# Two copies ahead of the gelu, and a step of the recurrence ahead of two maxima, in a macaron layer on eight cores

## The reference

```python
# x: (16, 4096, 1024); w1: (4096, 1024), w2: (1024, 4096), Wa, Wx: (1024, 1024)
def bitlinear(x, w, b):                  # int8 activations, ternary weights
    return einsum('bsd,fd->bsf', act_quant(rmsnorm(x)), weight_quant(w)) + b
def ffn(x):
    return bitlinear(gelu(bitlinear(x, w1, b1)), w2, b2)
def attn(x):                             # a gated linear recurrence
    rt, it = sigmoid(x @ Wa.T + ba), sigmoid(x @ Wx.T + bx)
    a = exp(-8 * softplus(-Lam) * rt)
    b = sqrt(1 - a * a) * (it * x)
    return scan(h = a * h + b)           # over the 4096 tokens
x = x + 0.5 * ffn(layernorm(x))
x = x + attn(layernorm(x))
x = x + 0.5 * ffn(layernorm(x))
```

## Time and profile before

| | us |
|---|---|
| three runs | 5005.6, 4954.83, 4643.77 |
| their median | 4954.83 |
| the profiled execution | 4643.38 |
| its span, slowest core (core 2) | 4641.8 |
| spans of its cores | 4631.0 to 4641.8 |
| PE busy in the span | 4225.2 (91%) |
| DVE busy | 3528.0 (76%) |
| ACT busy | 2790.7 (60%) |
| POOL busy | 972.4 (21%) |
| mean granted TensorE clock | 0.963 |

### The profile page before, as it was taken

One profiled execution on the slowest core, in us unless ns is written; L12 is line 12 of the kernel. 1 busy time (PEld: TensorE's weight loads), 2 busy tenths in 40 slices (PEclk: granted clock), 3 DMA queues, 4 the chain that ended last, 5 costly groups with the idle time before them and its releaser, 6 DMA issues.

```text
span 4641.8 us, 75615 instructions; the slowest of 8 cores (4631.0 to 4641.8 us)
## 1 busy us (share of the span) xinstructions
PE 4225.2 (91%) x23463; PEld 2242.4 (48%) x23463; DVE 3528.0 (76%) x4614; ACT 2790.7 (60%) x3464; POOL 972.4 (21%) x1541
## 2 busy tenths in 40 slices
PE   1699999999999989999999999999999999999999
PEld 0344455555555545454545445555555555444444
DVE  4888777777777777777777777777777777777786
ACT  4555666666666666666666666666666666555553
POOL 0122222222222222222221212222122221222221
PEclk9999999999999999999999999999999999999999
DMA  9455655556555555565555565555556555455555
GB/s 287 153 168 161 203 186 177 182 186 198 184 187 186 177 182 182 188 193 191 186 177 180 181 193 183 197 186 181 177 182 197 185 195 177 147 186 172 167 188 181
DMA packets 366185, 857.59 MB, mean 185 GB/s; under 512 B 39368, under 2 KB 45664, under 8 KB 365664
## 3 DMA queue, kind: packets, MB, share of 16 engines
q1 hardware_dynamic: 365792, 852.76, 56.5%
HBM read 740.41 MB, written 112.20 MB: 184 GB/s over the span
## 4 chain that ended last, share of the span: by engine, by line
PE 70%; DVE 16%; issue 7%; ACT 3%; DMA 2%; SPq 1%; DVEq 0%; POOL 0%; ACTq 0%; POOLq 0%
PE f_pm L486 29%; PE f_po L642 27%; PE aux L874 9%; DVE f_h L499 3%; PE aux L463 2%; DVE w2T L932 2%; DVE w2T L923 2%; ACT f_A L470 2%; DMA p_ring<-L_ffn_w 2%; PE aux L946 1%; DVE f_col L510 1%; PE aux L850 1%; DVE f_q L540 1%; SPq L62 1%; DVE f_col L435 1%
## 5 line engine op out<-in xcount | busy, mean ns | idle before, releaser
L486 PE MATMUL f_pm<-w1T,f_q1T 128*128 128x512 fp8e4 x8192 | 1837.6, 380 | 13.7 <-DVE f_h L499 4.7
L486 PEld LDWEIGHTS f_pm<-w1T,f_q1T 128*128 128x128 f16 x8192 | 795.0, 98 | 924.7 <-issue 24.1
L642 PE MATMUL f_po<-w_x,f_A 128*128 128x512 fp8e4 x4960 | 1161.9, 389 | 3.9 <-DMA w_x<-w2x 2.2
L505 ACT ACTIVATE f_h<-f_h 128x1024 f32<-128x1024 f32 x512 | 539.5, 1057 | 865.0 <-DVE f_h L499 859.6
L499 DVE SCALAR_TENSOR_TENSOR f_h<-f_pm,f_col,f_b1c 128x1024 f32<-128x1024 f32 x512 | 654.8, 1279 | 222.2 <-PE f_pm L486 217.1
L669 DVE SCALAR_TENSOR_TENSOR f_xb<-f_po,f_col,f_xb 128x512 f32<-128x512 f32 x496 | 370.1, 748 | 583.7 <-PE f_po L642 557.4
L642 PEld LDWEIGHTS f_po<-w_x,f_A 128*128 128x128 f16 x4960 | 498.2, 101 | 569.6 <-issue 60.4
L510 DVE TENSOR_REDUCE f_col<-f_h 128x1 f32<-128x1024 f32 x512 | 621.5, 1214 | 29.1 <-ACT f_h L505 17.1
L874 PE MATMUL aux<-w2T,g_w 128*128 128x256 bf16 x4096 | 536.0, 290 | 110.9 <-ACT f_A L470 110.9
L517 ACT ACTIVATE f_sqj<-f_h 128x1024 bf16<-128x1024 f32 x512 | 540.4, 1056 | 26.0
L874 PEld LDWEIGHTS aux<-w2T,g_w 128*128 128x128 bf16 x4096 | 418.6, 103 | 214.3 <-issue 119.2
(11 more groups left out here) (102 smaller groups left out, 3855.0 us busy)
## 6 DMA issues: line engine op xcount, KB each, us to landing
w_x<-w2x SPq DMA_DIRECT2D x1736, 256.0 KB, 5.3
g_w<-wg SPq DMA_DIRECT2D x256, 512.0 KB, 5.7
p_ring<-L_ffn_w SPq DMA_DIRECT2D x64, 512.0 KB, 16.4
f_xb<-L_attn_x SPq DMA_DIRECT2D x64, 512.0 KB, 6.1
xs<-f_xb SPq DMA_DIRECT2D x64, 512.0 KB, 6.4
g_xg<-xs SPq DMA_DIRECT2D x32, 1024.0 KB, 8.1
xs<-g_xg SPq DMA_DIRECT2D x32, 1024.0 KB, 5.2
f_xb<-xs SPq DMA_DIRECT2D x64, 512.0 KB, 5.6
```

The costliest lines, as they stand in the source:

```text
L486: a = put("tensor", lambda t, k=k, hf=hf, o=o: t.matmul(pm[i][:, hf * 512:(hf + 1) * 512], q1T[:, k * 128:(k + 1) * 128], w1T[:, o:o + 512 ...
L505: tj["gelu%d" % p] = put("scalar", lambda s: s.activation(hg[:, sl], hg[:, sl], AF.Gelu), waits=[ev])
L642: a = put("tensor", lambda t, k=k, c=c, w=w: t.matmul(po[:, bank * 512:(bank + 1) * 512], lhs[:, k * 128:(k + 1) * 128], w[:, c * 512:(c + ...
```

## The change

Three calls are moved in the loop over `j`. No instruction is added, removed or altered.

- `t2(pre, order[0])` stands before `evict1(cur, 1)`; it stood after it and after `recur(j, -4)`, which has VectorE work only. On TensorE its transposes follow `mm1(cur, 1)` as they did. On ScalarE its copy is ahead of gelu 1, where it was behind it.
- `t2(pre, order[1])` stands before `evict1(cur, 2)`; it stood after it, after `product_out(K, 3)` and after `gmax(cur, 1)`. On TensorE its transposes follow `mm1(cur, 2)` as they did. On ScalarE its copy is ahead of gelu 2, where it was behind it.
- `recur(j, -1)` stands before `gmax(cur, 2)`, `gmax(cur, 3)` and `scale2(cur)`, which are VectorE's alone. TensorE's and ScalarE's orders are as they were; on VectorE the addition of `g_tr_out` in stage 0 is ahead of the two maxima and the scale.

```diff
                         if cur is not None:
                             mm1(cur, 1)
+                        if pre is not None:
+                            t2(pre, order[0])
+                        if cur is not None:
                             evict1(cur, 1)
                         recur(j, -4)
-                        if pre is not None:
-                            t2(pre, order[0])
                         if nxt is not None:
                             quant1(nxt)
                         recur(j, -3)
...
                         if cur is not None:
                             gmax(cur, 0)
                             mm1(cur, 2)
+                        if pre is not None:
+                            t2(pre, order[1])
+                        if cur is not None:
                             evict1(cur, 2)
                         if odd:
                             product_out(K, 3)
                         if cur is not None:
                             gmax(cur, 1)
-                        if pre is not None:
-                            t2(pre, order[1])
-                        if cur is not None:
                             mm1(cur, 3)
                             evict1(cur, 3)
+                        recur(j, -1)
+                        if cur is not None:
                             gmax(cur, 2)
                             gmax(cur, 3)
                             scale2(cur)
-                        recur(j, -1)
```

## The result

The changed kernel takes 4369.8 us (median of four runs; three of them lie between 4368.5 and 4370.0), 0.941 of the kernel before, with a 95% interval of 0.9387 to 0.9432. The profiled execution took 4369.6 us, against 4643.4 us before: 273.8 us less, or 5.9%. The median of the four runs of before is 4799 us because two of them, like one of the changed kernel (4950.6 us, with a mean granted clock of 0.85 on four cores), ran at a lower clock, and no comparison here uses those.

The account below looks back on a forecast made before the run. TensorE was taken as the bound, losing time to waits and the lower clock behind them. Gains of 5.8 + 4.2 + 1.5 + 4.6 = 16.1 us a cycle, 16 cycles, 258 us: 4643 to 4385 us; 8-in-10 range 4320 to 4490.

Parts of the forecast that it names:

- the basis of the time: Whole kernel: gain subtracted from the profiled execution, 4643.4 us, the lowest run shown being 4643.8 and the median 4954.8 us.
- The bound and the two releasers: TensorE sets the pace; its idle time is mostly waiting for `aux` banks, released by ScalarE's copy or VectorE's addition.
- The copies: Stage 2: both copies ahead of their gelu gain 5.8 us (even) and 4.2 us (odd) a cycle, 160 us in all.
- What is late next: Stage 2 even: t1, then the bank of gate 5, each wait some 0.5 us for the tanh behind gelu 3.
- The new wait for the normalisation: Stage 0 even: TensorE's transposes at line 850 wait some 2.5 us for line 841, near 40 us in all.
- The echo behind the new wait: After stage 0 even's new wait, matmuls run at the lower clock and lose 1.7 us, leaving 1.5 of 3.2 us gain.
- Stage 0 odd: Earlier addition gains 3.3 us, vanished echo 1.7, less 0.4 for normalisation and second addition: 4.6 us a cycle.
- The queue of SyncE: Stage 0: four weight pieces behind the 1 MB store, costed at nothing; without cover up to 3 us a slot, 96 us.
- Sum: All terms together: 5.8 + 4.2 + 1.5 + 4.6 = 16.1 us a cycle, 258 us in 16 cycles, giving 4385 us.
- VectorE did not take stage 0 whole: Rival, chance 0.12: VectorE stays late in both stage 0 slots, only the copies' 160 us remain, 4483 us.
- No gelu became late: Rival, chance 0.03: gelu 1 and 2, now behind a 1.85 us copy, come late; at worst 4563 us.
- The clock did not fall in the dense stretch: Rival, chance 0.03: the chip grants less clock to a denser stream; slower, about 5340 us by the skill page's 13/16.

Follow-up runs that it names:

- kernels at 4293: Changed kernel with the recurrence's step also ahead of part 3's eviction and gelu, and two VectorE sums behind the normalisation in stage 0 even: 4292.6 to 4294.4 us.
- 4354 us: Changed kernel with the recurrence's step also ahead of the eviction and gelu of part 3: 4353.3 to 4355.4 us, ratio 0.938.

## Why the prediction was right, and where it was off

Slot by slot, from the starts of the first matmul at line 486 in the two timelines (one cycle of each, so each number is one reading):

| slot | before, us | after, us | gain | foretold |
|---|---|---|---|---|
| stage 2 odd | 40.88 | 36.61 | 4.27 | 4.2 |
| stage 0 even | 36.21 | 33.37 | 2.84 | 3.2 |
| stage 1 odd, with the echo | 35.73 | 36.70 | -0.97 | -1.7 |
| stage 2 even | 40.04 | 34.29 | 5.75 | 5.8 |
| stage 0 odd | 36.72 | 31.76 | 4.96 | 4.6 |
| stage 1 even | 32.27 | 32.28 | 0 | 0 |
| cycle | 221.85 | 205.01 | 16.8 | 16.1 |

- **The step that failed, the basis of the time**: the sum was laid on the profiled execution, 4643.4 us, and the distance to the runs shown was put at nothing. Their median was 4954.8 us, 6.7% above, and the prediction said only that "the rows can't say why". The range of 4320 to 4490 us has no term for it. The runs showed that the distance is real and does not cancel: the fourth run of the kernel before brought the median to 4799.4 us, the measured ratio of 0.941 makes 4516 us of that, above the range, and one run of the changed kernel took 4950.6 us. For an execution like the profiled one the sum holds: 5.6% less foretold, 5.9% measured. What sets one execution of a kernel apart from another stays open.
- **The bound and the two releasers**: right. The waits of the earlier trace rows were the lost time. Each was a reader of an `aux` bank that stood behind work it did not depend on.
- **The copies**: right in place and size, 160 us foretold, 164 measured by themselves. I credited both moves; the run with the second copy alone gives as much as both.
- **What is late next**: right. The 0.5 and 0.5 us for the tanh came as 0.47 and 0.35 us. The new wait for the normalisation, foretold at 2.5 us and 40 us in all, came as 2.28 and 36.6. VectorE's idle times of 0.52, 0.68 and 0.82 us closed as the sum had them.
- **The echo behind the new wait**: right in kind. It fell partly in stage 0 even (0.74 us of transposes) and partly in the next slot (0.97 us), together 1.7 us as foretold. The step's reason was wrong, though. I took the 2.45 us wait of stage 2 odd as proof that a wait of that length brings the lower level. The runs with four and eight more matmuls show that the same wait, with its length kept, has its echo in 15 of 15 cycles or in none. In the changed kernel 14 of 16 waits had it, and that is luck: by this alone the sum could have missed by up to 27 us.
- **Stage 0 odd**: the term was sized 0.36 us too low a cycle, 6 us. I had left 0.4 us for the normalisation and for the second addition, and no such wait appeared; the 0.19 us that is left of the first wait was already in the other terms.
- **The queue of SyncE**: the store with four weight pieces behind it cost nothing. TensorE waits 1.8 us in all for pieces, as before the change (2.2).
- **Sum**: 16.8 against 16.1 us a cycle, 269 against 258 us; some 4 us more lie outside the regular cycles. 4385 us foretold, 4370 measured.

The rivals: VectorE did not take stage 0 whole, but it took what was foretold of the even slots, and three of the four further gains were found in its order. No gelu became late; VectorE's wait of 17.1 us for gelu before the change is gone from its list. The clock did not fall in the dense stretch of the profiled execution. The Trainium skill, "TensorE: Matmul & The Clock Gate", section "Seeing it yourself", would have had it at 13/16; PE is busy for 588 of 598 us there, on eight cores, at 1.00.

## What to carry to other kernels

In a kernel whose engines run in order, look at every reader of a scarce buffer and ask what stands ahead of it that it does not need: here moving one copy past one gelu was worth 164 us, and moving one addition past two maxima 135 us by itself and 110 us on top of the copies, with not one instruction less. Follow the release one step further each time, since the next reader of the same bank (here the tanh, then the second addition) takes over part of the wait. And count a wait of TensorE together with what the clock does behind it.

## What the runs showed of the hardware

I had taken the lower clock level behind a wait to follow from the wait's length. For waits of 2.1 to 2.5 us it doesn't: 15 of 15 gates slow in the kernel before, 0 of 15 with four more matmuls in the cycle, 8 of 15 in the kernel with the step alone. That the moment at which the wait falls decides is my reading, not shown by itself. Here a kernel became 5 us faster through 14 us of useless work, and the gains of separate edits didn't add: 164 and 135 us apart, 274 together. Waits of 1.0 to 1.6 us left the clock at its upper level (the longest in the kernels at 4293 and 4354 us), and waits of 3.3 us and more always lowered it here.
